# Attention with routed experts on one core: routing in two chunks, maxima split ahead of the turning

## The chip, the cores and the metric

The kernel runs on one core of a Trainium2 chip. The metric is the device time of one execution in microseconds (us), the median of several runs. TensorE multiplies matrices, VectorE and ScalarE work elementwise, GpSimd does elementwise work and issues indirect DMAs, and SyncE's queue (SP) issues the plain DMAs.

## The reference

32 sequences of 128 rows and 512 columns. First a gated cross attention over channels, then a gated mixture of experts on each of the 4096 rows:

```python
x = x + tanh(g_xattn[0]) * xattn(_layernorm(x), ctx, Wq, bq, Wk, bk, Wv, bv)   # 8 heads of 16, 512 queries and keys
x = x + tanh(g_ffn[0]) * ffn(_layernorm(x), ...)
# ffn: h = _rmsnorm(x); probs = softmax(h @ router_w); topv, topi = top_k(probs, 2); topv /= sum(topv)
#      moe = sum over the two chosen of 8 experts of topv * (silu(h @ w_gate) * (h @ w_up)) @ w_down
#      sh  = the same with one shared expert for every row;   result moe + sh
```

## The kernel before, in words

**The attention loop.** `TURNS` is a software pipeline over the 32 batches b; a turn i has 32 steps s. In turn i TensorE computes the exponent's scores of batch i (`exp_scores`, L865), the scores from which batch i+1's row maxima are taken (`max_scores`, L843), the values of batch i (`values`, L896), a projection for a later batch (L820) and, from turn 3 on, turns tokens of batch i-3 and computes its router logits. VectorE takes one maximum every second step (`maximum`, L1112, 128x1024 from two PSUM banks, which TensorE may reuse only after it). ScalarE does one exponential a step (L1396) from one of the three banks of `turning`. GpSimd splits the projections into three bf16 parts (`split`, L652 to L655), normalises, makes tokens, and adds the attention (`add_attention`, L663 to L665). Each engine and queue runs its instructions in the order written.

**The maxima.** Batch b has 32 maxima a row: 8 heads by 4 blocks of 128 queries, in two halves of 16. When a half is found, `turn_maxima` (L852) turns it with a float32 identity into 16 rows of a bank of `turning`. VectorE then runs `maxima_rows`: L1121 writes the negated maximum as bf16, L1122 what that leaves out, both 16x128 from PSUM. `row` (L503) sends them to SBUF rows 48 and 49 of `q_stack`, one transfer for each part, where the score matmul adds them. `exp_scores` waits for both transfers before the first step of the half.

**SP's order in a turn.** The copies of the key's parts (`copy_parts`, L441, L445), the denominators (L459), `row(i, 1)`, further copies, the values (L452), the queries' copies, the reciprocals' store and broadcast load (L463, L469, landing as arena<-rden_d), `row(i + 1, 0)`, then loads and stores. GpSimd's `add_attention` waits for the broadcast; its next `split` comes after it, and SP's next copies after that.

**The routing.** `CHUNK` = 4 batches go through it together, N_CHUNKS = 8, in arrays of C = 32 columns. `choices` (12 VectorE steps, L1158 to L1172), one exponential, `count_choices` on TensorE (L905, L906), `take_counts` (L1177), and `places` (13 steps, L1187 to L1199). In the loop a step of these runs between two maxima, seven a turn. `scatter(b)` on GpSimd (L714) then writes the 128 rows' entries of batch b, 8 bytes each, at computed places of the table `map_d` in DRAM: two indirect DMAs, one for each choice. With four batches in a chunk, scatter(b) stands in turn b+10 ahead of `add_attention`; batches 21 to 23 stand together in turn 31, 24 to 27 after the loop's last tokens, 28 to 31 after the last chunk's places.

**The jobs.** After the loop come 103 jobs: 32 for the shared expert, then 71 tiles of routed rows. In each, TensorE turns the activation of the job before (L961), computes gate and up, then the former job's down product (L939). `source` (L498) loads a batch's turned tokens, in two buffers. Choices of the last chunk run in jobs 10 and 11, its places in jobs 14 and 15. GpSimd waits until all 64 scatters have landed, gathers the table (L755), and in job `TURN_AT` = 24 `turn_map` (L911) turns it on TensorE ahead of that job's other work. VectorE makes `ids` and `wts` of it, and GpSimd gathers the rows of routed tiles by them (L762). The first routed tile is turned at the end of job 31.

## Time and profile before

| | us |
|---|---|
| median of 3 runs | 1383.61 |
| lowest, highest | 1377.54, 1387.97 |
| the profiled execution | 1386.25 |
| its span | 1384.4 |

```profile
PE 1284.4 (93%) x12274; PEld 677.8 (49%) x12274; DVE 981.7 (71%) x1661; ACT 873.8 (63%) x1720; POOL 860.7 (62%) x1267
```

```profile
PE   4899998999999899999999888899999999999997
DVE  7888888999999899999998788556654333333332
ACT  2688887888888788788888677533334333333332
POOL 8666777677887788887887653541114555555553
```

The first line gives each engine's busy time and instructions; POOL is GpSimd, PE TensorE, DVE VectorE, ACT ScalarE. The others cut the span into 40 equal slices of 34.6 us, a digit being the busy share in tenths. The first 25 slices are the attention loop, the next four the shared expert's jobs, the rest the routed tiles.

### The profile page before, as it was taken

How to read it: one execution, taken by the hardware profiler on the slowest of the kernel's cores; microseconds unless marked ns; L12 is line 12 of the kernel's file. 1: busy time of each engine (PE TensorE's matmuls, PEld its weight loads, DVE VectorE, ACT ScalarE, POOL GpSimd, SP SyncE). 2: the span in 40 equal slices, each digit the busy share in tenths (PEclk: the TensorE clock that was granted, in tenths of full speed). 3: DMA queues.
4: the chain of work that ended last, by engine and by line, in shares of the span. 5: the costliest groups of instructions: out<-in, count | busy, mean ns of one | idle time of the engine just before them, and what ended most of it. 6: DMA issues, size and time to landing. Idle time of an engine off the chain costs nothing.

```text
span 1384.4 us, 34559 instructions
## 1 busy us (share of the span) xinstructions
PE 1284.4 (93%) x12274; PEld 677.8 (49%) x12274; DVE 981.7 (71%) x1661; ACT 873.8 (63%) x1720; POOL 860.7 (62%) x1267
## 2 busy tenths in 40 slices
PE   4899998999999899999999888899999999999997
PEld 1233333333333233333333222487788888888885
DVE  7888888999999899999998788556654333333332
ACT  2688887888888788788888677533334333333332
POOL 8666777677887788887887653541114555555553
PEclk8899999999999999999999999999999999999999
DMA  5545645645765576674665443465555898875665
GB/s 158 155 136 167 181 134 151 187 132 144 164 155 140 137 172 152 144 184 132 148 164 129 124 116 86 139 166 160 127 170 110 210 220 199 178 185 108 108 112 78
DMA packets 154467, 206.34 MB, mean 149 GB/s; under 512 B 35045, under 2 KB 84844, under 8 KB 154302
## 3 DMA queue, kind: packets, MB, share of 16 engines
q1 hardware_dynamic: 136046, 166.76, 44.6%
q0 software_dynamic: 18256, 37.38, 14.7%
q8 instruction: 103, 1.69, 0.6%
q14 instruction: 62, 0.51, 0.1%
HBM read 82.34 MB, written 61.94 MB: 104 GB/s over the span
## 4 chain that ended last, share of the span: by engine, by line
PE 40%; SPq 16%; issue 13%; POOL 10%; DVE 10%; DMA 8%; ACT 3%; POOLq 1%; DVEq 0%; ACTq 0%
PE m_banks L939 18%; SPq L445 7%; DVE row_max L1112 6%; PE bank L896 6%; PE bank L865 5%; PE m_banks L843 4%; DMA arena<-rden_d 4%; SPq L441 3%; PE bank L820 2%; POOL xs L762 2%; SPq L503 2%; ACT arena L1396 1%; SPq L459 1%; POOL arena L652 1%; SPq L452 1%
## 5 line engine op out<-in xcount | busy, mean ns | idle before, releaser
L1112 DVE TENSOR_REDUCE row_max<-m_banks 128x2 f32<-128x1024 f32 x512 | 614.1, 1222 | 71.8 <-PE m_banks L843 66.6
L1396 ACT ACTIVATE arena<-bank 128x512 f32<-128x512 f32 x1024 | 551.5, 606 | 76.2 <-PE bank L865 75.6
L865 PE MATMUL bank<-arena 112*32 112x512 bf16 x4096 | 332.6, 382 | 19.6 <-DMA arena<-m_rows 15.8
L896 PE MATMUL bank<-arena 128*32 128x512 f32 x2048 | 280.3, 598 | 1.7 <-ACT arena L1404 1.7
L865 PEld LDWEIGHTS bank<-arena 112*32 112x32 bf16 x4096 | 113.0, 95 | 280.4 <-ACT arena L1396 122.8
L774 POOL DMA_INDIRECT out<-xs,ids x71 | 112.3, 1582 | 172.4 <-ACT xs L1478 137.3
L843 PE MATMUL m_banks<-arena 48*128 48x512 bf16 x1024 | 176.0, 391 | 36.5 <-DVE row_max L1112 36.2
L939 PE MATMUL m_banks<-w_ring,h_hi 128*128 x568 | 183.1, 403 | 0.0
L1467 ACT ACTIVATE arena<-m_banks 128x256 f32<-128x256 f32 x103 | 39.5, 384 | 188.6 <-PE m_banks L939 188.6
L843 PEld LDWEIGHTS m_banks<-arena 48*128 48x128 bf16 x1024 | 40.2, 93 | 169.5 <-DVE row_max L1112 87.9
L1320 DVE TENSOR_TENSOR arena<-arena,m_banks 128x256 f32<-128x256 f32 x71 | 29.9, 421 | 116.4 <-ACT arena L1467 116.4
L939 PE MATMUL m_banks<-w_ring,h_lo 128*128 x284 | 111.7, 393 | 0.0
L939 PEld LDWEIGHTS m_banks<-w_ring,h_hi 128*128 128x128 f32 x568 | 101.4, 189 | 18.4
L1314 DVE TENSOR_TENSOR act_lo<-bank,act_hi 128x256 fp32r<-128x256 f32 x71 | 30.1, 424 | 96.7 <-ACT act_hi L1484 96.7
L762 POOL DMA_INDIRECT xs<-h_d,ids x71 | 70.2, 989 | 41.0 <-issue 21.0
L663 POOL TENSOR_TENSOR arena<-arena 128x512 f32<-128x512 f32 x32 | 41.0, 1281 | 87.9 <-DMA arena<-rden_d 81.9
L714 POOL DMA_INDIRECT map_d<-meta,slots x64 | 65.8, 1029 | 47.3 <-DVE slots L1199 30.9
L1478 ACT ACTIVATE xs<-m_banks,wts 128x512 f32<-128x512 f32 x71 | 48.8, 688 | 71.0 <-PE m_banks L939 71.0
L896 PEld LDWEIGHTS bank<-arena 128*32 128x32 f32 x2048 | 64.6, 109 | 51.2 <-issue 28.1
L1379 ACT ACTIVATE arena<-bank,bias 128x512 f32<-128x512 f32 x64 | 44.0, 688 | 71.8 <-PE bank L820 70.4
L939 PE MATMUL m_banks<-w_ring,act_hi 128*128 x284 | 87.5, 389 | 1.4 <-DVE act_lo L1314 1.4
L820 PE MATMUL bank<-arena 128*32 128x512 f32 x512 | 73.4, 647 | 15.2 <-POOL arena L643 10.4
(182 smaller groups left out, 2032.2 us busy)
## 6 DMA issues: line engine op xcount, KB each, us to landing
arena<-arena SPq DMA_DIRECT2D x256, 128.0 KB
arena<-arena SPq DMA_DIRECT2D x384, 64.0 KB
split_d<-staged SPq DMA_DIRECT2D x30, 512.0 KB, 6.9
w_ring<-split_d SPq DMA_DIRECT2D x60, 256.0 KB, 3.9
arena<-in_w SPq DMA_DIRECT2D x36, 256.0 KB, 7.0
arena<-in_ctx SPq DMA_DIRECT2D x32, 256.0 KB, 3.9
xs<-in_x SPq DMA_DIRECT2D x32, 256.0 KB, 4.4
arena<-rden_d SPq DMA_DIRECT2D x32, 256.0 KB
```

The costliest lines, as they stand in the source:

```text
L445: sp.dma_start(rows[:, a:HEADS:2, :], src[a:P:2, :]).then_inc(s_cp[n], DMA)
L714: nc.gpsimd.indirect_dma_start(map_d, bass.IndirectOffsetOnAxis(ap=slots[:, k, b:b + 1], axis=0), meta[:, k, b, :], None).then_inc(s_sc2, DMA)
L762: nc.gpsimd.indirect_dma_start(gathered[i % IN_RING], None, h_d, bass.IndirectOffsetOnAxis(ap=ids[:, i:i + 1], axis=0)).then_inc(s_got[i % ...
L774: nc.gpsimd.indirect_dma_start(out_d, bass.IndirectOffsetOnAxis(ap=ids[:, i:i + 1], axis=0), y_sb[i % OUT_RING], None, compute_op=ALU.add) ...
L820: last = nc.tensor.matmul(out[c, :], (wk, wq)[n][:, c], ctx_in[b % 2] if n == 0 else xn[b % 2], start=True, stop=True)
L843: nc.tensor.matmul(m_ps[pair % M_PAIRS][:, a, :], q_stack[b % 3][rows, h, qt * P:(qt + 1) * P], k_stack[b % 3][rows, h, :], start=True, st ...
L865: last = nc.tensor.matmul(out[c, :], k_stack[b % 3][0:SHIFTED, h, kt * P + c.start:kt * P + c.stop], q_stack[b % 3][0:SHIFTED, h, :], star ...
L896: last = nc.tensor.matmul(pv_ps[2 * DH * j:2 * DH * (j + 1), :], v_ones[b % 3][:, kt, GROUP * g + j, :], probs[pair % 3][:, j, :], start=( ...
L939: last = nc.tensor.matmul(out, v[:, c, :], weights(j, part, first_row + c), start=(c == 0 and n == 0), stop=(c == chunks - 1 and n == 2))
L1112: nc.vector.reduce_max(pair, m_ps[(STEPS * b + u) // 2 % M_PAIRS], AX_X).then_inc(s_mx, 1)
L1396: nc.scalar.activation(probs[group % 3][:, j, :], bank_of["scores", b, s], ACT.Exp, scale=float(DH) ** -0.5).then_inc(s_exp, 1)
L1478: nc.scalar.activation(y_sb[i % OUT_RING], Y_PS[j % 2], ACT.Copy, scale=wts[:, i:i + 1]).then_inc(s_yrt, 1)
```

## The change

Two things are changed together. The routing goes in chunks of 16 batches: `CHUNK` = 16, so C = 128 columns and two chunks. Chunk 0's choices are in turn 18, its counts in 19, its places in 20; scatters of batches 0 to 15 stand two to a turn (four DMAs) in turns 22 to 29. All of batches 16 to 31 (32 DMAs) come after the last places, in the jobs. `TURN_AT` becomes 27. The ranks are kept once and broadcast.

The maxima's parts are made by VectorE from `row_max` (128x16, SBUF) right after the last maximum of a half, into one 128x32 bf16 tile. One bf16 matmul turns both; ScalarE copies the 32x128 result to `m_rows` after step 19's or step 3's exponential, and one DMA takes both rows. Left out below: the same renaming of `wts[:]` and `ids[:]` to `wts` and `ids` where they are used.

```diff
--- before.py
+++ after.py
@@ -38,6 +38,7 @@
 HIGH_AT = (27, 31)
+PARTS_AT = (15, 31)
 MAX_AT = (19, 3)
...
 TURN_TOKENS_AT = 12
@@ -60,7 +61,7 @@
 LOADED = 2 * W_ROWS * DMA
-CHUNK = 4
+CHUNK = 16
 SPARES = 3
...
 QUIET_AT = 20
@@ -144,6 +145,7 @@
         wq, wk, wv = (a.take(P) for _ in range(3))
+        m_rows = [a.take(P // 2, BF16)[0:2 * GROUP * KT, :] for _ in range(2)]
         attention_end = a.at
...
@@ -154,7 +156,9 @@
         added_all = a.take(NT + 1)
-        a.take(2 * L - NT * EXPERTS - NT - 1)
+        ids = a.take(NT, I32)
+        wts = a.take(NT)
+        a.take(2 * L - NT * EXPERTS - 3 * NT - 1)
         assert a.at >= attention_end, (a.at, attention_end)
...
@@ -199,7 +203,8 @@
         row_max = [sb(f"row_max{i}", [P, HEADS * KT]) for i in range(2)]
-        m_rows = [sb(f"m_rows{i}", [GROUP * KT, 2, P], BF16) for i in range(2)]
+        m_parts = [sb(f"m_parts{i}", [P, 2 * GROUP * KT], BF16) for i in range(2)]
+        ident_b = sb("ident_b", [P, P], BF16)
...
         arg = sb("arg", [P, B])
@@ -211,11 +216,12 @@
         ones = sb("ones", [P, P], BF16)
-        route = sb("route", [P, 12 * C])
+        route = sb("route", [P, 8 * C + 5 * EXPERTS])
         a = Arena(route)
-        left, r_tmp, place, *pick = (a.take(C) for _ in range(5))
-        rank, restart = a.take(C), a.take(C)
+        r_tmp, place, *pick = (a.take(C) for _ in range(4))
+        rank, restart = a.take(EXPERTS), a.take(C)
         counts = a.take(2 * C)
+        left = counts[:, 0:C]
         top = a.take(8 * CHUNK).rearrange("p (n b) -> p n b", n=8)
...
         tile_p, map_of = a.take(1), a.take(1, I32)
@@ -228,8 +234,6 @@
         unused_map = logits[0:EXPERTS - 1, :].rearrange("p (s k) -> p s k", k=2)
-        ids = sb("ids", [P, NT], I32)
-        wts = sb("wts", [P, NT])
         tile_no = sb("tile_no", [P, NT])
...
         need_of = dead_stats.take(NT, I32)
@@ -278,6 +282,7 @@
         s_mx = sem("s_mx")
+        s_mp = sem("s_mp")
         s_mt = sem("s_mt")
...
         s_row = [sem(f"s_row{i}") for i in range(2)]
@@ -371,7 +376,7 @@
         MOMENTS_JOB = 6
-        TURN_AT = 24
+        TURN_AT = 27
...
         TURNS = range(-3, B)
@@ -499,9 +504,8 @@
                 sp.wait_ge(s_mr, 2 * b + half + 1)
-                for n in range(2):
-                    sp.dma_start(q_stack[b % 3][STACK + n:STACK + n + 1, half * GROUP:(half + 1) * GROUP, :],
-                                    m_rows[half][:, n, :]).then_inc(s_row[half], DMA)
+                sp.dma_start(q_stack[b % 3][STACK:STACK + 2, half * GROUP:(half + 1) * GROUP, :], m_rows[half]
+                             ).then_inc(s_row[half], DMA)
...
                 if is_b(i + 2):
@@ -625,6 +629,9 @@
                                     pattern=[[-1, P]], channel_multiplier=1).then_inc(s_setup, 1)
+            link(nc.gpsimd.memset(ident_b[:], 0.0))
+            nc.gpsimd.affine_select(out=ident_b[:], in_=ident_b[:], compare_op=ALU.not_equal, fill=1.0, base=0,
+                                    pattern=[[-1, P]], channel_multiplier=1).then_inc(s_setup, 1)
...
@@ -672,7 +679,7 @@
                     (unused_i, [[1, P]], 0, P),
-                    (by_token(rank).bitcast(I32), [[0, CHUNK], [-1, EXPERTS]], EXPERTS, 0),
+                    (rank.bitcast(I32), [[-1, EXPERTS]], EXPERTS, 0),
                     (region.bitcast(I32), [[REGION, EXPERTS]], 0, 0),
...
                     (tile_no[:].bitcast(I32), [[1, NT]], 0, 0),
@@ -733,8 +740,8 @@
                     staged_low(i + 2)
-                for b in range(B - 2 * CHUNK):
-                    if i == min(b + 10, B - 1):
+                for b in range(CHUNK):
+                    if i == CHUNK + 6 + b // 2:
                         scatter(b)
...
                     add_attention(i - 1)
@@ -748,7 +755,7 @@
                            channel_multiplier=0).then_inc(s_iota, 1)
-            for b in range(B - 2 * CHUNK, B):
+            for b in range(CHUNK, B):
                 scatter(b)
...
             pool.wait_ge(s_map_of, 1)
@@ -844,12 +851,11 @@
             def turn_maxima(b, half):
-                n = GROUP * KT
                 if b == 0 and half == 0:
-                    pe.wait_ge(s_setup, 1)
-                pe.wait_ge(s_mx, (STEPS * b + n * (half + 1)) // 2)
+                    pe.wait_ge(s_setup, 2)
+                pe.wait_ge(s_mp, 2 * b + half + 1)
                 out = take_bank(("maxima", b, half), s_mr, 2 * b + half + 1)
-                nc.tensor.matmul(out[0:n, 0:P], row_max[b % 2][:, n * half:n * (half + 1)], ident[:],
+                nc.tensor.matmul(out[0:2 * GROUP * KT, 0:P], m_parts[half][:], ident_b[:],
                                  start=True, stop=True).then_inc(s_mt, 1)
...
             def exp_scores(b, s):
@@ -857,7 +863,7 @@
                 if kt == 0 and j == 0:
-                    pe.wait_ge(s_row[g], 2 * DMA * (b + 1))
+                    pe.wait_ge(s_row[g], DMA * (b + 1))
                 if n == 0:
...
                 out = take_bank(("scores", b, s), s_exp, n + 1)
@@ -901,7 +907,7 @@
                 if c == 0:
-                    pe.wait_ge(s_setup, 3)
+                    pe.wait_ge(s_setup, 4)
                 nc.tensor.matmul(out[:, 0:C], before[:], chosen[:], start=True, stop=True)
...
@@ -997,8 +1003,8 @@
                         values(i, s // GROUP - 1)
-                    if s + 3 == COUNT_SLOT and i >= 7 and (i - 7) % CHUNK == 0:
-                        count_choices((i - 7) // CHUNK)
+                    if s + 3 == COUNT_SLOT and i > CHUNK and (i - 3) % CHUNK == 0:
+                        count_choices((i - 3) // CHUNK - 1)
                     if i == B - 1 and s == FIRST_JOB_AT:
...
@@ -1105,23 +1111,19 @@
                 dve.wait_ge(s_ms, STEPS * b + u + 2)
-                if u == 0 and b >= 2:
-                    dve.wait_ge(s_mt, 2 * (b - 2) + 2)
                 half, w = divmod(u // 2, GROUP * KT // 2)
...
-            def maxima_rows(b, half):
+            def maxima_parts(b, half):
                 n = GROUP * KT
-                turned = bank_of["maxima", b, half][0:n, 0:P]
-                dve.wait_ge(s_mt, 2 * b + half + 1)
+                found = row_max[b % 2][:, n * half:n * (half + 1)]
+                hi, lo = m_parts[half][:, 0:n], m_parts[half][:, n:2 * n]
+                dve.wait_ge(s_mx, (STEPS * b + n * (half + 1)) // 2)
                 if b:
-                    dve.wait_ge(s_row[half], 2 * DMA * b)
-                return chain(
-                    lambda: nc.vector.tensor_scalar(m_rows[half][:, 0, :], turned, -1.0, None, ALU.mult),
-                    lambda: nc.vector.scalar_tensor_tensor(m_rows[half][:, 1, :], turned, -1.0,
-                                                           m_rows[half][:, 0, :], ALU.mult, ALU.subtract
-                                                           ).then_inc(s_mr, 1))
+                    dve.wait_ge(s_mt, 2 * (b - 1) + half + 1)
+                link(nc.vector.tensor_scalar(hi, found, -1.0, None, ALU.mult))
+                nc.vector.scalar_tensor_tensor(lo, found, -1.0, hi, ALU.mult, ALU.subtract).then_inc(s_mp, 1)
...
             nc.vector.memset(middle_rows(k_stack[0]), TWO_ONES).then_inc(s_blank[0], 1)
@@ -1154,12 +1156,14 @@
+            ranks = rank.unsqueeze(1).broadcast_to([P, CHUNK, EXPERTS])
+
             def choose(k, p):
...
                         lambda: TT(by_token(r_tmp), by_token(p), each(top[:, k, :]), ALU.is_equal),
-                        lambda: TT(r_tmp, r_tmp, rank, ALU.mult),
+                        lambda: TT(by_token(r_tmp), by_token(r_tmp), ranks, ALU.mult),
                         lambda: nc.vector.reduce_max(top[:, 2, :], by_token(r_tmp), AX_X),
-                        lambda: TT(by_token(pick[k]), by_token(rank), each(top[:, 2, :]), ALU.is_equal))
+                        lambda: TT(by_token(pick[k]), ranks, each(top[:, 2, :]), ALU.is_equal))
...
                 own = logits[:, C * c:C * (c + 1)]
@@ -1227,12 +1231,10 @@
                 for s in range(STEPS):
-                    if s == MAX_AT[1] + 1 and is_b(i):
-                        run(maxima_rows(i, 1))
-                    if s == MAX_AT[0] + 1 and is_b(i + 1):
-                        run(maxima_rows(i + 1, 0))
                     if s % 2 == 0 and is_b(i + 1):
                         maximum(i + 1, s)
+                    if s in PARTS_AT and is_b(i + 1):
+                        maxima_parts(i + 1, PARTS_AT.index(s))
                     if s == RECIP_AT and is_b(i - 1):
...
                     if s == MOMENTS_AT and is_b(i + 5):
@@ -1241,14 +1243,14 @@
                         take_logits(i - 3)
-                    if s == QUIET_AT and i >= 6 and (i - 6) % CHUNK == 0:
-                        routed.append(choices((i - 6) // CHUNK))
-                    if s == QUIET_AT and i >= 8 and (i - 8) % CHUNK == 0:
-                        routed.append(places((i - 8) // CHUNK))
+                    if s == QUIET_AT and i > CHUNK and (i - 2) % CHUNK == 0:
+                        routed.append(choices((i - 2) // CHUNK - 1))
+                    if s == QUIET_AT and i > CHUNK and (i - 4) % CHUNK == 0:
+                        routed.append(places((i - 4) // CHUNK - 1))
                     if QUIET_AT <= s < QUIET_AT + 7:
                         routed = [steps for steps in routed if next(steps, steps) is not steps]
-                    if s == COUNT_SLOT and i >= 7 and (i - 7) % CHUNK == 0:
-                        take_counts((i - 7) // CHUNK)
+                    if s == COUNT_SLOT and i > CHUNK and (i - 3) % CHUNK == 0:
+                        take_counts((i - 3) // CHUNK - 1)
                     if i == B - 1 and s in SHARED_PARTS_AT:
...
                     if i == B - 1 and s == FIRST_TOKENS_AT:
@@ -1341,8 +1343,6 @@
                     add_shared(j - 1)
-                if j == 0:
-                    run(places(N_CHUNKS - 2))
                 if j == CHOICES_AT:
...
                     advance(last_choices, 7)
@@ -1396,6 +1396,12 @@
+            def take_maxima(b, half):
+                act_e.wait_ge(s_mt, 2 * b + half + 1)
+                if b:
+                    act_e.wait_ge(s_row[half], DMA * b)
+                nc.scalar.copy(m_rows[half], bank_of["maxima", b, half][0:2 * GROUP * KT, 0:P]).then_inc(s_mr, 1)
+
             def take_values(b, g):
...
                 if b:
@@ -1432,10 +1438,14 @@
                         exponential(i, s)
+                    if s == MAX_AT[1] and is_b(i):
+                        take_maxima(i, 1)
+                    if s == MAX_AT[0] and is_b(i + 1):
+                        take_maxima(i + 1, 0)
                     if s in HIGH_AT and is_b(i + 3):
                         high_part(i + 3, HIGH_AT.index(s))
-                    if s == EXP_SLOT and i >= 7 and (i - 7) % CHUNK == 0:
-                        exponentials((i - 7) // CHUNK)
+                    if s == EXP_SLOT and i > CHUNK and (i - 3) % CHUNK == 0:
+                        exponentials((i - 3) // CHUNK - 1)
                     if s == STAGE_AT and 0 <= i + 2 < len(STAGED):
...
                     if s == TURN_TOKENS_AT + 1 and is_b(i - 3):
```

## Rows read from the trace of the kernel before

**Rows 1.** The chain of work that ended last, 118 to 170 us: start, us, what.

```profile
123.12 0.55 SPq L445
...
127.59 0.59 SPq L503
...
137.32 3.75 DMA arena<-rden_d
...
148.34 0.55 SPq L445
```

**Rows 2.** The same view, 500 to 560 us.

```profile
514.95 0.27 PE bank L852
...
524.15 0.34 DVE arena L1104
...
532.34 0.99 DVE route L1160
...
550.40 0.34 DVE arena L1104
```

**Rows 3.** VectorE's groups by line and shape, whole span: count, busy us, mean ns.

```profile
L1122 DVE SCALAR_TENSOR_TENSOR m_rows<-bank,m_rows 16x128 bf16<-16x128 f32 x64 | 17.8, 278 | 2.2
L1121 DVE TENSOR_SCALAR m_rows<-bank 16x128 bf16<-16x128 f32 x64 | 17.2, 269 | 1.3 <-PE bank L852 1.3
L1160 DVE TENSOR_TENSOR route<-route 128x32 f32<-128x32 f32 x16 | 6.7, 417 | 0.3
```

**Rows 4.** The page's costliest groups: one of ScalarE's.

```profile
L1467 ACT ACTIVATE arena<-m_banks 128x256 f32<-128x256 f32 x103 | 39.5, 384 | 188.6 <-PE m_banks L939 188.6
```

**Rows 5.** The tile m_rows: ns min/median/max, first and last start.

```profile
L503 SPq DMA_DIRECT2D arena<-m_rows x128: 549/584/2532, 43.5 to 864.2; - x128
```

**Rows 6.** GpSimd's timeline, 539 to 593 us: start, us, instruction, idle before it.

```profile
539.41 1.16 POOL L652 TENSOR_TENSOR arena<-arena 128x512 bf16<-128x512 f32 x1
...
552.37 0.34 POOL L632 TENSOR_SCALAR newton<-r,arg 128x1 f32<-128x1 f32 x1 [1.44 <-DVE r L1060]
...
559.67 1.08 POOL L714 DMA_INDIRECT map_d<-meta,slots  x1 [0.15 <-issue]
561.06 0.97 POOL L714 DMA_INDIRECT map_d<-meta,slots  x1 [0.30 <-issue]
...
565.67 1.16 POOL L652 TENSOR_TENSOR arena<-arena 128x512 bf16<-128x512 f32 x1
```

**Rows 7.** GpSimd's timeline, 961 to 1003 us: last chunk's eight scatters, then the gathers.

```profile
961.52 1.49 POOL L714 DMA_INDIRECT map_d<-meta,slots  x1 [30.95 <-DVE slots L1199]
...
971.18 0.97 POOL L714 DMA_INDIRECT map_d<-meta,slots  x1 [0.30 <-issue]
981.37 1.84 POOL L755 DMA_INDIRECT slot_map<-map_d,route  x1 [9.23 <-DMA map_d<-meta,slots]
1002.91 1.00 POOL L762 DMA_INDIRECT xs<-h_d,ids  x1 [19.70 <-DVE wts L1366]
```

**Rows 8.** The tile slot_map: its one gather's time to landing.

```profile
DMA to landing us min/median/max: 8.0/8.0/8.0
```

**Rows 9.** Loads of line 498, issued 983 to 1003 us.

```profile
DMA to landing us min/median/max: 2.6/2.7/5.1
```

**Rows 10.** The same for the load issued at 972.4 us.

```profile
DMA to landing us min/median/max: 8.9/8.9/8.9
```

**Rows 11.** The same for the two issued between 920 and 930 us.

```profile
DMA to landing us min/median/max: 5.0/6.6/8.2
```

**Rows 12.** TensorE's timeline: the table's turning in job 24, job 27's first work.

```profile
996.11 0.34 PE L911 MATMUL bank<-ident,slot_map 71*128 71x71 f32 x2
...
1009.32 0.38 PE L961 MATMUL bank<-ident,early_act 128*128 128x128 f32 x2
```

**Rows 13.** Engines by windows: window, us, busy of each, PEclk, DMA share, GB/s.

```profile
780.00:784.00 4.00, 4.00 (x34) 1.40 (x31) 2.55 (x5) 2.10 (x5) 3.76 (x5) 0.62 0.73 226
```

**Rows 14.** The chain that ended last, 880 to 900 us.

```profile
884.71 2.78 SPq L452
```

8 lines of the change are left out of this document (4 added, 4 removed).

## The prediction

> **What bounds the kernel now.** I read the page first: TensorE is busy 93% of the span, but the attention loop, 25 of the 40 slices, has three other engines at 7 to 9 tenths, so no share of busy time says what an edit is worth. I then read the chain of waits turn by turn. In the early turns it doesn't run through TensorE at all. It is a ring of SP and GpSimd: SP issues the copies, both maxima's rows and the reciprocals one behind the other, the broadcast of the reciprocals takes 3.75 us to land, GpSimd adds the attention and splits, and SP may go on. One round is 148.34 - 123.12 = 25.2 us, and each row transfer holds 0.59 us of it and some 0.04 us between issues [rows 1]. In most middle turns the chain is TensorE's matmuls and VectorE's maxima in turn. From one reciprocal of the denominators to the next it is 550.40 - 524.15 = 26.25 us, with routing steps in it such as one of 0.99 us, and two turnings of maxima a turn at 0.27 us [rows 2]. Over the loop a turn is about (864.2 - 43.5) / 31.4 = 26.1 us, the divisor being the turns between the first row transfer, late in turn -1, and the last, early in turn 31 [rows 5]. So two rings lie some 1 us apart, and an edit that shortens one gains no more than down to the other.
>
> After the loop TensorE goes from job to job. A job is (1009.32 - 996.29) / 3 = 4.34 us, where 996.29 is the turning of the table plus its own 0.18 us [rows 12]. What can stop it there is order: `turn_map` stands ahead of everything else in its job, so a table that is late stops TensorE altogether. Before, job 24 didn't wait.
>
> **The maxima's edit.** VectorE loses L1121 and L1122: 64 each at 0.269 and 0.278 us, 35 us, 1.1 us a turn [rows 3]. In their place come two steps of 128x16 from SBUF, not in the trace. Between nothing and the old price I take 0.17 us each, above the middle since a fixed part must remain with an eighth of the columns, so 0.7 us a turn, and a gain of 0.4. They lie between the half's last maximum and TensorE's turning, but that turning is four score matmuls further on, which cover them. TensorE's two turnings of 0.27 us become two bf16 ones, at 0 to 0.27 us, say 0.1: 0.3 us a turn. ScalarE gets two copies of 32x128. Its nearest row is 0.384 us for 128x256 [rows 4], so at most 0.77 us a turn, I take 0.55. Behind such a copy stand all later exponentials, for whose banks TensorE waits; the page has ScalarE at 7 or 8 tenths in these slices, and this idle time hides most of it. SP loses one of two transfers for each half, 2 x 0.63 us a turn, of which the one in the ring, `row(i, 1)`, is worth 0.63 us. The other lies behind the reciprocals' load and is worth nothing there. If one transfer of 32 rows cost as much as two of 16, the gain would be nil. The second identity costs GpSimd under 1 us at the start, ahead of a wait for VectorE that covers most of it.
>
> **The routing's edit in the loop.** Seven of eight chunks were in the loop, so nearly every turn had six or seven routing steps on VectorE. Now only turns 18 to 21 have them, four times as wide. The steps stood between maxima, on the chain: the 128x32 product costs 0.417 us on average [rows 3] and up to 0.99 [rows 2]; I count 1.5 us a turn on the chain of middle turns. With 0.3 us of turnings and 0.4 us of parts, the TensorE and VectorE ring would go from 26.25 to about 24.1 us. The SP and GpSimd ring sits at 25.2 - 0.63 = 24.6 us, more whenever the broadcast takes over 3.75 us, and the copies on ScalarE cost something. I take 25.3 us for turns 5 to 21: 17 turns x 1.0 = 17 us gained, and 5 x 0.6 = 3 us for turns 0 to 4, which had no routing.
>
> In turns 22 to 29 GpSimd gets in the way. From one split to the next it takes 565.67 - 539.41 = 26.26 us, of which 1.44 us is a wait for VectorE, so it needs 24.8 us with two scatter DMAs in it [rows 6]. Two more, at (971.18 - 961.52) / 7 = 1.38 us a piece [rows 7], make 27.6 us; behind them stands `add_attention`, and behind that the split for which SP waits. Against 26.3 that is 1.3 us in turns where the weights staged need both of GpSimd's steps, less in the others: 8 x 0.9 = 7 us lost. The loop's balance is a gain of 17 + 3 - 7 = 13 us. Its bounds are 30 us (24.6 us in every turn up to 21, and none lost later) and nothing.
>
> **The jobs.** The six scatters at the end of the loop and the eight after it are gone from there. Loads issued among the second burst took 5.0 and 8.2 us [rows 11] against 2.7 in a calm stretch [rows 9], and an issue of SP on the chain was held 2.78 us [rows 14]. I count 4 us gained before job 14, between 0 and 6.
>
> Now the 32 DMAs after the last places. The trace has eight of them alone. Issued from 961.52 to 971.18 us, they weren't all landed until 981.37, when the table's gather could start [rows 7]: the landing is 9.2 us behind the last issue. A load in a calm stretch lands in 2.6 us [rows 9], so eight took 19.85 us, of which the first needed about 1.49 + 2.6 = 4.1, and the seven others (19.85 - 4.1) / 7 = 2.25 us each, though issued 1.38 apart. A load issued among them took 8.9 us [rows 10]. So I take it that these 8-byte writes land one DMA behind another at 2.25 us, and that faster issuing doesn't help. The Trainium skill ("DMA: Bandwidth & Descriptors", Specifications) says that transfers under 512 B make the DMA engine read and write back. That speaks against this change, the trace's 2.25 us against 1.38 agrees, and the rule alone would add nothing to the sum.
>
> Then, from the first of the last chunk's scatters: 0.8 us for wider places steps, 4.1 us for the first, 31 x 2.25 = 69.8 us, and 8.0 us for the table's gather [rows 8], 82.7 us. Job 27 begins 1009.32 - 961.52 = 47.8 us after the first scatter [rows 7, 12]. TensorE therefore stands still for 82.7 - 47.8 = 34.9 us. Nothing covers it; what follows only shifts. Loads that are slow before job 27 eat from the same wait. After `turn_map` the chain has enough room: the first gather was issued 1002.91 - 996.11 = 6.8 us behind it [rows 7, 12], and the first routed tile is needed four jobs, 17.4 us, behind. So 10.6 us are left for landing, more than the 8.0 of the table's. After so long an idle time I expect one spell at half clock, as in the window at 780 us with PEclk 0.62, which is 1.2 GHz for most of it [rows 13]: 1.7 us. The stall's bounds are these. At issue pace, 1.38 us, it is 0.8 + 4.1 + 42.8 + 8.0 - 47.8 = 7.9 us; if the burst's pace were 19.85 / 8 = 2.5 us, 42.6.
>
> **The sum** is against the profiled execution's span of 1384.4 us: -13 - 4 + 34.9 + 1.7 = +19.6, giving 1404.0. That execution was 1386.25 us in all, 2.6 above the median of 1383.6, so the median after is 1383.6 + 19.6 = 1403, 1.4% slower. A change of 1%, 13.8 us, is about what a measurement of this kernel can tell.
>
> **Rivals.** (A) The writes land at the pace of their issue: the waits before were other traffic's doing, since stores and loads ran beside the eight. The stall is 7.9 us, and 1383.6 - 13 - 4 + 7.9 = 1374. The Trainium skill ("DMA: Bandwidth & Descriptors", Anatomy of one DMA) has about 2 us of fixed cost for each DMA, mostly the write's receipt, and the transfers pipelined; by that the result would be this one. Against it are the 9.2 us behind the last issue [rows 7]. It decides for faster where a landing costs under (17 - 1.7 - 0.8 - 4.1 - 8.0 + 47.8) / 31 = 1.62 us. Chance 0.17.
>
> (B) The stall comes, but the loop gains its full 30 us, because both rings fall to 24.6 us and GpSimd's scatters fall into its wait for the broadcast. 1383.6 - 30 - 4 + 34.9 + 1.7 = 1386: within 1%. For it speaks that turn 3, without routing, took 25.2 us [rows 1]. Against it are GpSimd's 24.8 us [rows 6]. Chance 0.20.
>
> (C) The loop gains nothing: four scatters a turn slow the broadcasts and copies as they did the load at 972 us [rows 10], and ScalarE's copies in the middle of the exponentials cost what the routing gave back. 1383.6 - 4 + 34.9 + 1.7 = 1416. Chance 0.13.
>
> My forecast, 1396 to 1410, has 0.50. The range over the cases is 1374 to 1418: it takes in A's and C's own values. Slower by over 1% (above 1397.4) takes most of the forecast's share and C: 0.57. Within 1% are B, most of A and a low end of the forecast: 0.33. Faster is the rest of A with a loop that gains more: 0.10.
>
> **What would show it.** In the profile after: TensorE idle some 35 us ahead of `turn_map`'s two turnings, released by the table's gather; GpSimd's gather of the table waiting for the landing of map_d some 30 us behind its last scatter (8 in case A); turns 5 to 21 at 25.3 us by the row transfers' starts, turns 22 to 29 at or above 26.5; single row transfers of about 0.6 us; ScalarE's new copy near 0.28 us. The prediction is wrong if the table's wait is under 15 us, which kills the drain, or if the last row transfer's start has come forward by more than 25 us, which makes the loop's gain the larger term.

## The result and the profile after

| | before | after |
|---|---|---|
| median, in runs on one chip | 1389.06 us (1377.54 to 1397.88, 20 runs) | 1396.72 us (1384.1 to 1409.11, 20 runs) |
| the profiled execution | 1386.25 us | 1393.62 us |
| its span | 1384.4 us | 1391.7 us |

The ratio is 1.0055, with an interval of 1.0032 to 1.0077: half a per cent slower, which is within 1%. The prediction had 1.4% slower, with 0.57 on slower by over 1% and 0.33 on within 1%.

The page after, busy time and the 40 slices, now of 34.8 us:

```profile
PE 1275.4 (92%) x12198; PEld 659.9 (47%) x12198; DVE 956.7 (69%) x1499; ACT 882.3 (63%) x1778; POOL 858.8 (62%) x1269
...
PE   4899999999999999898888879999899999999997
...
DVE  6999988989989989898878768367454333333332
ACT  2688888888888888788878758433324333333332
POOL 8676777777867777568887653212614555555553
```

VectorE lost 25 us of work and 162 instructions and the kernel did not get faster. TensorE's slices show where: slices 3 to 16 are now all 9s, where two were 8 before; then come six 8s and a 7 from slice 17 (at 557 us) to 24, where before the 8s began in slice 23.

To see it by turns I use ScalarE's exponentials, one for each step, 32 a turn: in a window from the first of turn 5 to the first of turn 18 there are 13 x 32 + 1 = 417, and the row's first and last starts are the two turns' beginnings. Columns: count, ns min/median/max, first and last start. Before, for turns 5 to 17, 18 to 21, 22 to 29, and all:

```profile
L1396 ACT ACTIVATE arena<-bank x417: 588/603/641, 169.3 to 513.7; 128x512 f32<-128x512 f32 x139
L1396 ACT ACTIVATE arena<-bank x129: 588/604/638, 513.7 to 618.6; 128x512 f32<-128x512 f32 x129
L1396 ACT ACTIVATE arena<-bank x257: 588/600/640, 618.6 to 834.4; 128x512 f32<-128x512 f32 x129
L1396 ACT ACTIVATE arena<-bank x1024: 587/602/641, 46.9 to 880.5; 128x512 f32<-128x512 f32 x171
```

The same of after:

```profile
L1396 ACT ACTIVATE arena<-bank x417: 588/603/638, 170.5 to 497.9; 128x512 f32<-128x512 f32 x139
L1396 ACT ACTIVATE arena<-bank x129: 579/602/637, 497.9 to 609.6; 128x512 f32<-128x512 f32 x129
L1396 ACT ACTIVATE arena<-bank x257: 589/599/639, 609.6 to 832.9; 128x512 f32<-128x512 f32 x129
L1396 ACT ACTIVATE arena<-bank x1024: 579/601/639, 47.9 to 878.7; 128x512 f32<-128x512 f32 x171
```

Turns 5 to 17 went from 344.4 to 327.4 us: 17.0 gained, 1.3 a turn. Turns 18 to 21, which now hold all of chunk 0's routing steps, went from 104.9 to 111.7: 6.8 lost. Turns 22 to 29, with four scatter DMAs each, went from 215.8 to 223.3: 7.5 lost. The first exponential is 1.0 us later, turns 0 to 4 cost 0.2 more, and the loop ends 1.8 us earlier in all.

These are sums of one trace each. Five of the kernels below (e3, e4, e5, e7, e8) have after's loop up to the turn at which their edit begins, and so show what such a sum is worth: turns 0 to 4 took 121.3 to 123.0 us in these and after, turns 5 to 17 took 327.4 to 329.1, turns 18 to 21 took 108.8 to 111.7 (without e7), and turns 22 to 29 took 221.1 in e4 and 227.7 in e5, against 223.3. Differences smaller than these spreads, the 0.2 us above among them, say nothing.

Then the jobs. TensorE's turning of the activation, from job 14 to job 27 (27 matmuls: two in a job), before and, in the second fence, after:

```profile
L961 PE MATMUL bank<-ident,early_act x27: 270/271/328, 950.1 to 1009.3; 128*128 128x128 f32 x27
```

```profile
L967 PE MATMUL bank<-ident,early_act x27: 270/272/461, 948.3 to 1016.7; 128*128 128x128 f32 x27
```

59.2 us became 68.4: 9.2 lost. What follows job 27 kept its length (363.9 us to the last job in either trace). So the span's +7.3 is -1.8 + 9.2 with 0.1 of rounding.

GpSimd's timeline after, the 32 scatter DMAs and the table's gather (answers [rows 7]); L721 is the scatter, L762 the gather:

```profile
960.85 1.57 POOL L721 DMA_INDIRECT map_d<-meta,slots  x1 [44.07 <-DVE slots L1203]
...
1001.35 0.97 POOL L721 DMA_INDIRECT map_d<-meta,slots  x1 [0.30 <-issue]
1009.57 1.85 POOL L762 DMA_INDIRECT slot_map<-map_d,route  x1 [7.25 <-DMA map_d<-meta,slots]
```

The scatters are issued (1001.35 - 960.85) / 31 = 1.31 us apart, and the gather may start 7.25 us behind the last: less than the 9.23 us behind only eight of them. What TensorE and ScalarE waited for in this stretch, from the list of waits of 950 to 1040 us (total, times, longest), from the groups of the whole span, and last the landing times of the loads of turned tokens (L503, issued 958 to 1005 us, eight of them; answers [rows 9 to 11]):

```profile
ACT early_hi L1507 <- DMA arena<-ht_d: 18.3, 8, 6.2
...
L917 PE MATMUL bank<-ident,slot_map 71*128 71x71 f32 x2 | 0.5, 313 | 0.8 <-DMA slot_map<-map_d,route 0.8
```

```profile
DMA to landing us min/median/max: 2.6/8.8/12.6
```

TensorE's first turning of the table waited 1.3 us in its weight load and 0.8 in the matmul, not 35. But it was late already: jobs 20, 22 and 23 took 7.0 us longer than before, since their loads took up to 12.6 us. Of the rest, 1.3 us are in job 26, at whose end the table is turned, and 1.1 in jobs 15 to 17.

Last, the edit of the maxima. The groups of after that answer [rows 3] and [rows 5] are these (busy us, mean ns, idle time before); the one transfer took 687 ns where two of 584 had been:

```profile
L1125 DVE TENSOR_SCALAR m_parts<-row_max 128x16 bf16<-128x16 f32 x64 | 28.1, 439 | 1.6 <-DVE half_i L1064 0.4
L1126 DVE SCALAR_TENSOR_TENSOR m_parts<-row_max,m_parts 128x16 bf16<-128x16 f32 x64 | 19.5, 305 | 2.2
L1403 ACT CAST arena<-bank 32x128 bf16<-32x128 f32 x64 | 15.5, 242 | 0.7 <-PE bank L858 0.6
L858 PE MATMUL bank<-ident_b,m_parts 128*32 128x128 bf16 x64 | 14.1, 220 | 21.5 <-DVE arena L1103 14.1 <-ACT arena L1396 3.6 <-DVE m_parts L1126 3.1
```

```profile
L507 SPq DMA_DIRECT2D arena<-arena x64: 658/687/771, 43.7 to 861.8; - x64
```

The two parts steps have an eighth of the old ones' columns, and take 47.6 us together where those took 35.0.

### The profile page after: what moved, and what is told of

Read it like the earlier page. It is cut to its first block, busy times and chain, and to the rows that moved or that the text cites. A ratio compares the mean times of both kernels' runs of the same rounds, so it can differ in the third digit from the quotient of the medians.

```text
span 1391.7 us, 34191 instructions
## 1 busy us (share of the span) xinstructions
PE 1275.4 (92%) x12198; PEld 659.9 (47%) x12198; DVE 956.7 (69%) x1499; ACT 882.3 (63%) x1778; POOL 858.8 (62%) x1269
## 3 DMA queue, kind: packets, MB, share of 16 engines
q8 instruction: 103, 1.69, 0.6%
## 4 chain that ended last, share of the span: by engine, by line
PE 40%; issue 18%; DVE 16%; POOL 12%; DMA 6%; SPq 5%; ACT 2%; POOLq 1%; DVEq 0%; ACTq 0%
PE m_banks L945 12%; DVE row_max L1116 10%; PE bank L902 8%; PE bank L871 8%; PE m_banks L850 5%; POOL map_d L721 3%; POOL xs L769 3%; PE bank L827 2%; SPq L450 2%; DMA out<-xs,arena 2%; PE bank L833 2%; DMA arena<-arena 2%; ACT arena L1396 1%; DVE m_parts L1125 1%; DMA arena<-rden_d 1%
## 5 line engine op out<-in xcount | busy, mean ns | idle before, releaser
L871 PE MATMUL bank<-arena 112*32 112x512 bf16 x4096 | 327.0, 385 | 23.4 <-DMA arena<-arena 15.8
L902 PE MATMUL bank<-arena 128*32 128x512 f32 x2048 | 271.4, 601 | 1.3 <-ACT arena L1410 1.1
L871 PEld LDWEIGHTS bank<-arena 112*32 112x32 bf16 x4096 | 102.5, 95 | 300.5 <-ACT arena L1396 142.1
L781 POOL DMA_INDIRECT out<-xs,arena x71 | 112.2, 1581 | 160.1 <-ACT xs L1488 123.1
L945 PE MATMUL m_banks<-w_ring,h_lo 128*128 x284 | 111.7, 393 | 0.0
L721 POOL DMA_INDIRECT map_d<-meta,slots x64 | 63.8, 996 | 62.4 <-DVE slots L1203 44.1
L1488 ACT ACTIVATE xs<-m_banks,arena 128x512 f32<-128x512 f32 x71 | 48.8, 688 | 71.0 <-PE m_banks L945 71.0
L639 POOL TENSOR_SCALAR newton<-r,arg 128x1 f32<-128x1 f32 x96 | 33.4, 348 | 96.5 <-DVE r L1066 89.5
L769 POOL DMA_INDIRECT xs<-h_d,arena x71 | 70.2, 988 | 32.6 <-issue 21.0
L827 PE MATMUL bank<-arena 128*32 128x512 f32 x512 | 73.4, 647 | 16.6 <-POOL arena L650 11.2
L659 POOL TENSOR_TENSOR arena<-arena 128x512 bf16<-128x512 f32 x62 | 72.1, 1163 | 19.8 <-ACT arena L1388 10.8
```

Source lines behind the costliest of these rows:

```text
L659: nc.gpsimd.tensor_tensor(mid, proj[n], hi, ALU.subtract).then_inc(s_part, 1)
L721: nc.gpsimd.indirect_dma_start(map_d, bass.IndirectOffsetOnAxis(ap=slots[:, k, b:b + 1], axis=0), meta[:, k, b, :], None).then_inc(s_sc2, DMA)
L769: nc.gpsimd.indirect_dma_start(gathered[i % IN_RING], None, h_d, bass.IndirectOffsetOnAxis(ap=ids[:, i:i + 1], axis=0)).then_inc(s_got[i % ...
L781: nc.gpsimd.indirect_dma_start(out_d, bass.IndirectOffsetOnAxis(ap=ids[:, i:i + 1], axis=0), y_sb[i % OUT_RING], None, compute_op=ALU.add) ...
L827: last = nc.tensor.matmul(out[c, :], (wk, wq)[n][:, c], ctx_in[b % 2] if n == 0 else xn[b % 2], start=True, stop=True)
L871: last = nc.tensor.matmul(out[c, :], k_stack[b % 3][0:SHIFTED, h, kt * P + c.start:kt * P + c.stop], q_stack[b % 3][0:SHIFTED, h, :], star ...
```

## The experiments

### The maxima's edit alone (e1)

Before, with the parts made ahead of the bf16 turning, ScalarE's copy and the one transfer; routing untouched.

```diff
-                    if s == MAX_AT[1] + 1 and is_b(i):
-                        run(maxima_rows(i, 1))
-                    if s == MAX_AT[0] + 1 and is_b(i + 1):
-                        run(maxima_rows(i + 1, 0))
+                    if s in PARTS_AT and is_b(i + 1):
+                        maxima_parts(i + 1, PARTS_AT.index(s))
```

Expected: 

> The kernel before with the maxima's edit alone (chunks of 4 batches, table turned in job 24). Theory S (both edits shorten the loop, each by its own ring): turns 5 to 17 fall from 26.4 us to about 25.7 and the later ones by about 0.6 too, in all 15 to 20 us less, no change after the loop: 1.2% faster. Rival R (the steps of the routing were what made turns 5 to 17 long, and the maxima's edit is hidden): within 0.3% of before. Rival M (all of the gain of 1.3 us a turn is the maxima's edit): turns 5 to 17 at 25.1 us, in all 30 us less, 2.2% faster.

Measured: 1399.72 us (10 runs) against 1387.02, ratio 1.0099 (1.0064 to 1.0134): slower, which no theory had. Turns 5 to 17 took 350.3 us (344.4 before) and the loop ended 12.0 us later. Two timelines, VectorE's and GpSimd's, show the kind of thing that happens:

```profile
573.69 1.09 DVE L1124 TENSOR_SCALAR m_parts<-row_max 128x16 bf16<-128x16 f32 x1
574.81 1.08 DVE L1125 SCALAR_TENSOR_TENSOR m_parts<-row_max,m_parts 128x16 bf16<-128x16 f32 x1
```

```profile
573.59 1.16 POOL L658 TENSOR_TENSOR arena<-arena 128x512 bf16<-128x512 f32 x1
574.70 1.16 POOL L659 TENSOR_TENSOR arena<-arena 128x512 f32<-128x512 f32 x1
```

Each of these two parts steps lasts until GpSimd's instruction is over. Of the 64 instances of the first step in this trace, 33 begin while GpSimd has no elementwise instruction under way, and all 33 take 174 to 176 ns. 26 begin inside a 128x512 instruction of its `split`, take 0.82 us on average (0.24 to 1.17), and end 0.03 us after it. The other five begin inside other 128x512 instructions and take 0.17 to 0.64. The old steps read PSUM and took 0.269 to 0.279 us whatever GpSimd did. The Trainium skill ("SBUF — State Buffer", SBUF: two separate sides) describes a port pair that VectorE and GpSimd share as an exclusive lock: a VectorE instruction with two SBUF inputs or in a two-port mode and a GpSimd instruction (against two SBUF inputs, one that reads SBUF) exclude each other for their whole length. The trace agrees, with 174 ns against up to 1166; the first step has one SBUF input, and no run here shows in which mode it works.

### The routing's edit alone (e2)

After, with the maxima's edit undone: chunks of 16, the old `maxima_rows`.

```diff
-CHUNK = 4
+CHUNK = 16
...
-        TURN_AT = 24
+        TURN_AT = 27
```

Expected: 

> The changed kernel with the maxima's edit undone: two chunks of 16 batches, table turned in job 27, rows made from the turned maxima by VectorE, two transfers a half. Theory S: turns 5 to 17 at about 25.8 us, turns 18 to 21 about 7 us longer in all than before, turns 22 to 29 about 8 us longer, jobs 14 to 27 about 9 us longer: 1.0 to 1.5% slower than before. Rival R: turns 5 to 17 at 25.1 us as with both edits, so 0.5% slower, as the changed kernel. Rival M: turns 5 to 17 unchanged at 26.4 us: 2% slower.

Measured: 1405.61 us (6 runs), ratio 1.0141 (1.0090 to 1.0192). Turns 5 to 17 took 333.9 us (10.5 less than before), 18 to 21 109.9 (5.0 more), 22 to 29 230.8 (15.0 more), jobs 14 to 27 70.1. The total is theory S's, but turns 22 to 29 lost 15 us where it had 8. So each half alone is slower than both together, 1.0% and 1.4% against 0.55%: the halves help each other. It isn't by a shorter undisturbed turn: e2, with two transfers, has five of turns 5 to 17 at 24.91 or 24.92 us, where after's shortest are 24.97. Its other turns are the longer ones, up to 28.0 us where after's turns 5 to 17 reach 25.9. Which of the maxima's changes does that, no run here separates.

### The loop's scatters left out (e3)

```diff
-                for b in range(CHUNK):
-                    if i == CHUNK + 6 + b // 2:
-                        scatter(b)
```

Expected: 

> The changed kernel without the 32 scatter DMAs of turns 22 to 29; the table's entries of those rows keep their starting values, so their experts' part is left out of the result while the number of tiles stays. Theory G (four scatters a turn are what makes turns 22 to 29 long, by GpSimd's time and by the slow transfers beside them): these eight turns fall from 223 us in all to about 205, since turns without routing or scatters took 25.1 to 25.4, and the half-clock spells there go; about 15 us (1.1%) faster than the changed kernel, 0.5% faster than before. Rival L (the late turns are long by other work, the loads of weights and tokens): they stay above 215 us.

Measured: 1369.5 us, ratio 0.988 (0.9816 to 0.9945). Its exponentials in turns 22 to 29:

```profile
L1394 ACT ACTIVATE arena<-bank x257: 587/603/638, 607.9 to 805.9; 128x512 f32<-128x512 f32 x129
```

198.0 us against 223.3: the scatters cost 25 us of the loop, theory G with some 7 us more than it had. Five of the eight turns are then at 24.97 us, two at 25.03 and 25.21, and turn 29 takes 22.8. The burst in the jobs, unchanged, cost the same (70.3 us from job 14 to 27). Here TensorE's weight load waited 6.5 us for the table, beside ScalarE's 15.8 us of waits for late loads: the two delays cover each other, and which of them shows differs from trace to trace.

### Chunks of eight, both edits (e6)

```diff
-CHUNK = 16
+CHUNK = 8
...
-        TURN_AT = 27
+        TURN_AT = 26
...
-                for b in range(CHUNK):
-                    if i == CHUNK + 6 + b // 2:
+                for b in range(B - CHUNK - 6):
+                    if i == CHUNK + 6 + b:
                         scatter(b)
```

Expected: 

> Both edits with chunks of 8 batches: four chunks, one scatter(b) a turn from turn 14, six batches' scatters after the loop ahead of the last chunk and 16 DMAs behind the last places, table turned in job 26. Theory S: turns without routing at 25.1 us, those with it (10 to 13, 18 to 21, 26 to 29) under 1 us longer since the steps are half as wide as in the changed kernel, no turn with four scatters; jobs 14 to 26 about 3 us longer than before: 15 us less than before in all, 1% faster. Rival W (what costs is that steps meet GpSimd's instructions, whatever their width): 12 turns each 1.5 us longer, and the total is within 0.5% of before.

Measured: 1378.24 us (1373.74 to 1384.59, 12 runs) against 1387.02, ratio 0.9943 (0.9913 to 0.9973): faster than both kernels. Its exponentials in turns 22 to 29:

```profile
L1396 ACT ACTIVATE arena<-bank x257: 587/603/638, 618.0 to 825.8; 128x512 f32<-128x512 f32 x129
```

Turns 5 to 17 (338.6 us) lose 11.2 to after, since chunk 0's steps now stand there, but turns 22 to 29 take 207.8 instead of 223.3, and jobs 14 to 27 take 60.1 instead of 68.4, with a burst of 16 DMAs instead of 32. Its table's gather waited 7.86 us behind the last scatter. The total lies between the two theories, and the turns speak for W: the twelve with routing steps take 27.4 us on average, 2.5 above a turn without, where S had under 1 and W had 1.5.

### The tail's scatters left out (e4), or made reads (e5)

e4 leaves out the 32 DMAs in the jobs; e5 puts a gather of the same entries for each.

```diff
-            for b in range(CHUNK, B):
-                scatter(b)
-            pool.wait_ge(s_sc2, 2 * B * DMA)
+            pool.wait_ge(s_sc2, 2 * CHUNK * DMA)
```

```diff
+            for b in range(CHUNK, B):
+                for k in range(2):
+                    nc.gpsimd.indirect_dma_start(slot_map[:, 2 * b + k, :], None, map_d,
+                        bass.IndirectOffsetOnAxis(ap=slots[:, k, b:b + 1], axis=0)).then_inc(s_sc2, DMA)
```

Expected of e4: 

> The changed kernel without the 32 scatter DMAs behind the last places; the entries of the later 16 batches keep their starting values and are left out of the experts' part. Theory D (in the jobs the scatters act through the loads beside them, which land in 7 to 13 us where a calm one takes 2.6, and TensorE waits in jobs 20, 22 and 23): jobs 14 to 27 go from 68.4 back to 59 to 60 us, the loads stay under 5 us. Rival O (the loss is the order, a table that is late by the issue time alone): the same total, so the next run tells the two apart. Either way about 9 us less than the changed kernel.

Expected of e5: 

> The changed kernel with the 32 scatter DMAs behind the last places turned into gathers of the same 8-byte entries: as many instructions of GpSimd, reads of DRAM in place of writes; the later 16 batches are left out of the experts' part. Theory D with small writes as the cause: the loads beside them land in under 5 us, jobs 20 to 23 take 4.4 us each, and what is left is the wait ahead of the table's turning, some 2 us: jobs 14 to 27 about 61 us. Rival Q (any 32 indirect DMAs crowd the queues): loads at 7 to 13 us again, 68 us.

Measured: e4 took 1385.6 us (8 runs), ratio 1.0027 (0.9992 to 1.0061), with jobs 14 to 27 at 59.2 us, to the tenth the time before, and its loads landing in 2.6 us (median; longest 3.1; of 11 loads the trace has the landing of five). So the burst of 32 costs these jobs 9.2 us, theory D. The whole time shows less of it: e4 lies 0.28% below after, 4 us, and the intervals leave room for 9. e5 took 1417.09 us (2 runs), ratio 1.0211 (1.0050 to 1.0372), with jobs 14 to 27 at 91.7 us, which neither theory had. Its reads landed sooner than the writes: the table's gather waited 1.69 us behind the last. But in the middle of the burst ScalarE stood for 22.9 us, and with it everything but GpSimd, and the trace names no releaser. ScalarE's timeline, and GpSimd's at the table's gather:

```profile
986.21 0.62 ACT L1513 CAST early_hi<-arena 128x512 fp32r<-128x512 f32 x1
1009.76 0.38 ACT L1483 ACTIVATE arena<-m_banks 128x256 f32<-128x256 f32 x1 [22.92 <-remote]
```

```profile
1006.58 1.81 POOL L767 DMA_INDIRECT slot_map<-map_d,route  x1 [1.69 <-DMA slot_map<-map_d,slots]
```

I have no cause for it that a run shows. It ended 3 us after the burst's last transfers had landed. What ScalarE waited for is the semaphore of TensorE's gate and up products: by the trace these matmuls ended at 981.6 us, and the semaphore rose at 1009.7. It was there again in the two kernels of the next section, though their 32 DMAs in the jobs are after's own writes, and not in e2, e3 and e11, whose traces list no such waits above the smallest, nor in after, where they sum to 4.2 us. So it isn't the reading that does it. Another thing sets these kernels apart: e4, e5, e7 and e8 were measured on one chip, and e1, e2, e3, e6, e9, e10 and e11 on three others. All four have such waits (e4, e5 and e8 in turns 23 to 28 too, beside the loop's indirect DMAs; in e4 the longest is 4.3 us) and none of the seven has one. Whether the chip makes them, no run shows, since no kernel with such a stall was measured on another. e5 doesn't say what the kind of transfer costs.

### The loop's scatters made reads (e8), and chunk 0's routing steps out too (e7)

e8 replaces chunk 0's scatters with gathers, as e5 did for chunk 1. e7 is e3 with VectorE's choices and places of chunk 0 cut to three short steps:

```diff
+                if c == 0:
+                    return chain(lambda: nc.vector.memset(top[:, 3, :], 0.0),
+                                 lambda: nc.vector.memset(chosen[:], 0.0).then_inc(s_ch, 1))
```

Expected of e8: 

> The changed kernel with the 32 scatter DMAs of turns 22 to 29 turned into gathers of the same entries: GpSimd's time stays, the small writes to DRAM go; the earlier 16 batches are left out of the experts' part. Theory W (the writes slow the transfers that the loop waits for): turns 22 to 29 fall from 223 us to 200 to 206. Rival G (GpSimd's 5 us a turn, in front of the adding of the attention): they stay at 218 to 225.

Expected of e7: 

> As the run without the loop's scatters, and without the first chunk's steps of choices and places in turns 18 to 21 (constants stand in their place; the earlier 16 batches are left out of the experts' part). Theory P (the wide steps are long because they meet GpSimd's instructions on SBUF): these four turns fall from 108.8 us to 4 x 25.0 = 100 us. Rival C (it is the half-clock spell and the exponential or counts): they stay over 105.

Measured for e8: turns 22 to 29 took 832.1 - 608.9 = 223.2 us, as with the writes (223.3 in after, 221.1 in e4 on the same chip): rival G. That they are 8-byte writes costs nothing that shows beside the spread of these sums. What is left, and what both kernels share, are four indirect DMAs ahead of `add_attention`; whether it is GpSimd's time for them or their transfers that costs, no run separates. For e7, turns 18 to 21:

```profile
L1400 ACT ACTIVATE arena<-bank x129: 588/605/637, 497.1 to 598.2; 128x512 f32<-128x512 f32 x129
```

101.1 us against e3's 108.8, and 111.7 in after: the wide steps cost 8 to 10 us in four turns, theory P. Both kernels' whole times (1410.4 and 1380.06 us, ratios 1.0163 and 0.9986) contain the stall told above (jobs 14 to 27 at 89.7 and 89.0 us), so only their turns are used.

### Chunks of eight with the old maxima (e9)

e6 with the maxima's edit undone.

Expected: 

> Chunks of eight, one scatter a turn, table turned in job 26, as in the run of 1378.24 us, but with the maxima's parts made from PSUM after the turning, as before the change. Theory S (the maxima's edit gains where VectorE has no routing steps and loses beside them; with chunks of eight most turns have none): worse than 1378.24 by some 8 us, about 1386; turns 22 to 29 at some 212 us against 207.9. Rival M (the edit costs VectorE about as much in any turn, as it did alone, 12 us over the loop): about 1366. Rival N (the two cancel): 1378, within 0.3%.

Measured: 1380.85 us (12 runs) against 1379.76, ratio 1.0001 (0.9969 to 1.0033), so 0.6% above e6's ratio, some 8 us. Turns 22 to 29 took 210.7 us (207.9 in e6), and the last exponential stood at 877.7 us, in e6 at 870.3. The maxima's edit, 12 us worse in before's routing, is 7 us better where most turns have no routing steps: theory S, at its size, though the two ratios' intervals still touch. The turns show the two sides of it: the twelve with routing steps took 321.0 us in e9 and 329.1 in e6, so the edit costs 8 us there, and the other eighteen of turns 0 to 29 took 465.2 and 449.5, so it gains 16.

### The parts steps left out (e10 on e1, e11 on after)

```diff
-                pe.wait_ge(s_mp, 2 * b + half + 1)
+                pe.wait_ge(s_mx, (STEPS * b + GROUP * KT * (half + 1)) // 2)
...
-                link(nc.vector.tensor_scalar(hi, found, -1.0, None, ALU.mult))
-                nc.vector.scalar_tensor_tensor(lo, found, -1.0, hi, ALU.mult, ALU.subtract).then_inc(s_mp, 1)
+                if b == 0:
+                    nc.vector.memset(m_parts[half][:], 0.0).then_inc(s_mp, 1)
```

Expected of e10: 

> The maxima's edit alone, as in the run of 1399.72 us, with VectorE's two parts steps left out of it (m_parts is zero throughout, so the exponentials are taken without their maxima; all transfers, turnings and ScalarE's copies stay). Theory P (the parts steps, 128x16 from SBUF at 453 and 369 ns while GpSimd works, are what made the edit slower): turns 5 to 17 fall from 350.3 to about 338 us, the loop ends at about 868 instead of 893.1, and the time is about 1375. Rival Q (ScalarE's copies behind the exponentials, and what waits for their banks, made it slower): turns 5 to 17 stay at 347 to 350, and the time stays above 1393. Between the two, 1385 or so, both have a part.

Expected of e11: 

> The changed kernel with VectorE's two parts steps left out (m_parts is zero throughout, so the exponentials are taken without their maxima; all transfers, turnings and ScalarE's copies stay). Theory F (turns 5 to 17 already stand at a floor of 24.97 to 25.3 us that the parts steps don't touch; they cost where VectorE also has routing steps or is late): turns 5 to 17 stay at 325 to 328 us, turns 18 to 21 fall from 111.6 to some 105, turns 22 to 29 from 223.3 to some 218, the time to about 1385. Rival A (the parts steps cost on the chain in every turn, 34 us over the loop as in the maxima's edit alone): turns 5 to 17 fall to 315 or less, the time to about 1365. Rival Z (they cost nothing here): within 0.3% of the changed kernel's 1.0055 times the kernel before.

Measured: e10 took 1363.68 us (6 runs), ratio 0.9881 (0.9836 to 0.9925), where e1 had 1.0099; e11 1388.38 us (12 runs), ratio 1.0033 (1.0004 to 1.0061), where after has 1.0055: e10 is theory P, and goes beyond it (turns 5 to 17 at 333.6 us), while the whole time of e11 alone doesn't exclude rival Z, and only its trace speaks for F. All exponentials of e10, and then of e11 (e1's last began at 892.5 us, after's at 878.7):

```profile
L1391 ACT ACTIVATE arena<-bank x1024: 577/603/638, 46.7 to 858.3; 128x512 f32<-128x512 f32 x171
```

```profile
L1392 ACT ACTIVATE arena<-bank x1024: 578/603/637, 46.7 to 866.8; 128x512 f32<-128x512 f32 x171
```

Beside before's routing the two steps cost 34.2 us of the loop, 1.07 a turn (they are busy for 1.64 a turn, part of it hidden). Everything else of the maxima's edit (one transfer, bf16 turning, ScalarE's copy, no PSUM steps) is thus worth some 22 us, since 858.3 is 22.2 below before's 880.5. Beside chunks of sixteen they cost 11.9 us: 1.2 before the first exponential, 2.7 in turns 0 to 4, 4.2 in turns 18 to 21 and 4.1 in turns 22 to 29, but next to nothing in the sum of turns 5 to 17 (327.2 us). Each of these parts by itself is hardly larger than the spread between traces of one loop, so their split is rough. Theory F, though its floor isn't one: the undisturbed turns got shorter. Two such turns of after and two of e11:

```profile
L1396 ACT ACTIVATE arena<-bank x65: 589/607/638, 195.6 to 245.6; 128x512 f32<-128x512 f32 x65
```

```profile
L1392 ACT ACTIVATE arena<-bank x65: 588/605/637, 166.7 to 215.9; 128x512 f32<-128x512 f32 x65
```

25.0 us a turn against 24.6. What bounds such a turn is read from the chain that ended last in it. For turn 8 of e2 (24.91 us) and turn 7 of after (24.97):

```profile
by line: SPq L447 23.9%; DMA arena<-rden_d 14.9%; SPq L443 12.2%; POOL xs L667 10.3%; issue 5.9%; POOL arena L665 5.2%; SPq L461 4.8%; POOL arena L657 4.7%; SPq L505 4.7%; POOL arena L654 4.6%; POOL arena L655 4.5%; SPq L454 4.5%; POOL aren
```

```profile
by line: PE bank L902 21.6%; PE bank L871 18.3%; DVE row_max L1116 14.8%; PE m_banks L850 12.8%; issue 11.0%; DVE m_parts L1125 4.9%; PE bank L833 4.0%; ACT arena L1396 4.0%; PE bank L827 4.0%; ACT arena L1388 2.0%; PE bank L858 1.7%; DVE a
```

In e2 it is the ring of SP and GpSimd, with two transfers a half; in turn 5 of e11 (24.58 us) it is the same ring with one, SP's copies L450 alone being 27.6% of it. In after it is TensorE with VectorE, and a parts step stands in it. Other turns of e11 took that back (turn 17 has 27.58 us); why, I didn't follow. And in the jobs e11 gave away 3 us more than after (71.5 us from job 14 to 27, in which TensorE waited up to 3.9 us for the table), and 2.5 more in job 27.

## Why the prediction was right in its range and wrong in its terms

The sum was -13 - 4 + 34.9 + 1.7 = +19.6 us. Measured in the profiled executions: -1.8 + 0 + 9.2 for the first three, +7.3 in all. Large errors of both signs partly cancelled. That the time lies in the range is luck. The median of 1396.72 us even falls into the forecast's 1396 to 1410, but only because the kernel before measured 1389.06 beside it, 5.5 us above the median that I started from; 1383.6 times 1.0055 is 1391.2. What came is a result within 1%, which I had given mainly to rivals B and A, and by neither's terms: B's loop was to gain 30 us and gained 1.8, A's was to gain 13.

**The stall: mis-sized, 34.9 for 9.2, and it came in another form.** I read the 9.23 us between the last scatter and the gather as a queue that grows, since the first costs 4.1 us and the other seven made up 15.75. It is a lag that doesn't grow with their number. It was 9.23, 9.16 and 7.15 us behind eight DMAs (before, e1, e10), 7.86 and 6.67 behind sixteen (e6, e9), and 7.25, 7.49, 7.28 and 8.12 behind 32 (after, e2, e3, e11); in e7 and e8, where the engines stood, it was 4.99 and 4.41. By my formula the pace is (1009.57 - 960.85 - 4.1) / 31 = 1.44 us, against my 2.25 and the issue's 1.31: rival A's mechanism, to which I had given 0.17. The rule that I named with it, a fixed cost of each DMA (the Trainium skill, "DMA: Bandwidth & Descriptors", Anatomy of one DMA), is what the trace shows in kind; its 2 us isn't, since 7.25 us passed behind the last issue. From one burst of one size the two couldn't be told apart, and I should have left both at even chances.

Rival A's price of 7.9 us was close to 9.2, but TensorE lost 7.0 of the 9.2 in jobs 20, 22 and 23, to loads of up to 12.6 us (the step "loads that are slow before job 27 eat from the same wait", which I named and didn't price). Had the loads been calm, job 27 would have begun at 948.3 + 59.2 = 1007.5 us and waited for the table until 1016.3, so 8.8 us: about the same. e4 shows that the burst causes both.

**The parts steps: 0.17 us predicted, 0.439 and 0.305 measured.** The fixed part I guessed is exact, 174 ns, when GpSimd is idle. What I left out is that these steps, unlike those they replace, take both operand and result from SBUF beside an engine at 7 to 8 tenths. I had bounded the price by "the old price", 0.27, as if a smaller tile couldn't cost more. And they aren't covered by four score matmuls: TensorE's turning waited for them, and what stands behind them on VectorE, the next maximum, is on the chain. That turned my -3 us of turns 0 to 4 into +0.2; e11 has 120.0 us there against 122.7 after (121.3 to 123.0 with its loop), which is most of the -3.

**Turns 5 to 21: 17 predicted, 10.2 measured.** Up to turn 17 the gain was 17.0 us and the turns 25.2 on average, against my 25.3. The steps of turns 18 to 21 cost more than I gave them: I priced all these turns alike, forgetting the four that now hold the work. VectorE's timeline of turn 20 (the maxima between left out):

```profile
568.66 0.85 DVE L1191 TENSOR_SCALAR route<-route 128x16 f32<-128x16 f32 x1
...
571.17 1.20 DVE L1194 TENSOR_TENSOR route<-route 128x8 f32<-128x8 f32 x1
...
573.54 1.32 DVE L1195 TENSOR_TENSOR_SCAN route<-route 128x128 f32<-128x128 f32 x1
574.90 1.15 DVE L1196 COPY route<-route 128x8 f32<-128x8 f32 x1
```

GpSimd's at the same time:

```profile
571.06 1.28 POOL L670 TENSOR_TENSOR arena<-arena 128x512 f32<-128x512 f32 x1 [1.58 <-DMA arena<-rden_d]
...
573.30 1.28 POOL L672 TENSOR_TENSOR xs<-xs,arena 128x512 f32<-128x512 f32 x1
574.87 1.15 POOL L659 TENSOR_TENSOR arena<-arena 128x512 bf16<-128x512 f32 x1 [0.28 <-ACT arena L1388]
```

The same lines in the jobs, for chunk 1, where GpSimd has nothing to do:

```profile
953.96 0.18 DVE L1191 TENSOR_SCALAR route<-route 128x16 f32<-128x16 f32 x1
...
954.67 0.17 DVE L1194 TENSOR_TENSOR route<-route 128x8 f32<-128x8 f32 x1
954.88 0.42 DVE L1195 TENSOR_TENSOR_SCAN route<-route 128x128 f32<-128x128 f32 x1
955.34 0.17 DVE L1196 COPY route<-route 128x8 f32<-128x8 f32 x1
```

4.5 us for four steps that take 0.9 alone. It isn't the width of the steps that costs most; it is the neighbour, and a step that waits for it holds the maximum behind it. TensorE then waits 2.82 us for the maximum, and the granted clock falls. The engines by windows, columns as in [rows 13]:

```profile
576.00:584.00 8.00, 6.64 (x42) 1.63 (x46) 5.58 (x13) 3.25 (x6) 4.24 (x5) 0.57 0.17 45
996.00:1000.00 4.00, 3.60 (x10) 2.92 (x11) 2.00 (x5) 0.61 (x3) 3.15 (x3) 0.57 0.76 83
```

Turn 20 took 31.7 us. I had one spell at half clock for 1.7 us; these two windows have a mean of 0.57, so 1.2 GHz for most of them. Before the first TensorE had waited for VectorE, before the second for late loads. What they cost by themselves I haven't measured.

**Turns 22 to 29: right in their sum.** 27.6 us a turn from GpSimd's work, so 7 us lost, was the prediction; 27.9 and 7.5 were measured. e3 shows it is the scatters, e8 that it isn't their being writes. That GpSimd's time makes the turn isn't shown: the eight turns run from 25.3 to 32.0 us, GpSimd itself was idle for 13.6 us of them ahead of the reciprocals' broadcast, and TensorE waited up to 6.4 us for a transfer of the maxima's rows, which it never did in these turns of e3.

**SP's ring: right in size by two errors, and not the floor.** I had 25.2 - 0.63 = 24.6 us. The ring shows in e2 with two transfers at 24.91 us, not 25.2, and in e11 with one at 24.58, so the transfer was worth 0.33 us, where 2 x 0.624 - 0.73 = 0.52 would follow from its rows. In after the undisturbed turn is 24.97 us and its chain TensorE and VectorE, which I had at 24.1: the other ring stands above SP's, with the parts steps in it.

**The jobs before 14: 4 predicted, 0 measured.** Job 1 is 1.6 us shorter, as the places of the chunk before last are gone; the wider choices make jobs 11 and 12 longer by 0.7 and 0.9.

**Small terms.** ScalarE's copy 0.242 us (0.28 predicted). The 64 turnings keep TensorE busy for 14.1 us, where the old ones, two overlapping matmuls of 0.27 us each, took 24.7: 0.33 us a turn saved, 0.3 predicted. The start is 1.0 us later, where I had the second identity at nearly nothing. My sign of failure, a table's wait under 15 us, was met, and it names the step that failed.

## What to carry over

A short VectorE step whose operands and result are in SBUF has no price of its own beside a busy GpSimd: 0.17 us alone, up to 1.2 behind one 128x512 instruction in these traces. Reading it from PSUM (0.27 us) can be the cheaper way, and where such steps must stand in SBUF, few of them matter more than small ones; placing them where GpSimd waits should help, which no run here tried. A lag behind a burst of DMAs isn't a price for each: before scaling it up, look for a second burst of another length. And when work that was spread over a loop is gathered, price the turns that receive it by themselves; chunks of eight with one scatter a turn, between the two designs, beat both (0.9943 of before, after 1.0055).

## What the runs showed of the hardware

- 8-byte scatters of 128 entries landed 6.7 to 9.2 us behind the last of 8, 16 or 32 of them in nine kernels, without growing with the number, and 4.4 and 5.0 behind it in the two in which the other engines stood (e8, e7); gathers of the same entries 1.7 us behind (e5). While 32 such writes ran in after, seven of eight loads issued beside them took 7.0 to 12.6 us instead of 2.6.
- VectorE's 128x16 steps between SBUF tiles took 174 ns or up to 1982 ns, the 16x128 ones from PSUM 269 to 279 ns always (before). The longest, at 688.55 us in after, began inside a scatter of GpSimd's (688.23 to 689.18 us) and ended with the 128x512 multiplication behind it (689.20 to 690.49).
- A stall of some 20 us in the burst of 32 indirect DMAs, with no releaser in the trace, in three (e5, e7, e8) of the seven kernels with a burst of 32 there (these, e2, e3, e11 and after). The three were measured on one chip, e2, e3 and e11 on two others. Its cause is open.
